# Layer 2's first gather moved ahead of its additions, radial features on another queue, and one ring for all stages

## The reference

```
h = relu(layernorm(x)); x = x + gat(h)         # layer 0: attention over in-edges and self loops
h = relu(layernorm(x)); x = x + sage_sage(h)   # layer 1: two SAGE convolutions (means over in-edges)
h = relu(layernorm(x)); x = x + layer2(h)
h = relu(layernorm(x)); x = x + relational(h)  # layer 3: typed messages, summed by dst

def layer2(h):
    radial, conical = h[:, :16], h[:, 16:32]
    rows, cols = concat([i, j]), concat([j, i])      # every edge in both directions
    agg = segment_sum(conical[cols], rows) / max(degree(rows), 1)
    return relu(concat([radial, agg]) @ W1 + b1) @ W2 + b2   # 32 -> 128 -> 32
```

## Time and profile before

| | |
|---|---|
| median of 3 runs | 4690.81 us |
| profiled execution | 4694.78 us |
| its span | 4693.0 us |
| GpSimd busy | 3469.0 us (74%) |
| VectorE busy | 2870.1 us (61%) |
| TensorE matmul busy | 2328.5 us (50%) |
| ScalarE busy | 958.4 us (20%) |
| stage f, from its first load to g's first gather | 3002.5 to 3604.6 us |

### The profile page before, as it was taken

One profiled execution on the slowest core, in us unless ns is written; L12 is line 12 of the kernel. 1 busy time (PEld: TensorE's weight loads), 2 busy tenths in 40 slices (PEclk: granted clock), 3 DMA queues, 4 the chain that ended last, 5 costly groups with the idle time before them and its releaser, 6 DMA issues. The chain is left out here.

```text
span 4693.0 us, 30595 instructions
## 1 busy us (share of the span) xinstructions
PE 2328.5 (50%) x8870; PEld 1409.5 (30%) x8870; DVE 2870.1 (61%) x3600; ACT 958.4 (20%) x1485; POOL 3469.0 (74%) x3151
## 2 busy tenths in 40 slices
PE   7820067775777730000622331177764677666562
PEld 3410034443555420000622331022221444443331
DVE  8866177775888756666311110166665899988783
ACT  0012022221445421111000000144442111111110
POOL 7777677774777747776588888777774777777777
PEclk9865555555989875555655555588886787877776
DMA  1035244441444432222122222344442111110100
GB/s 29 12 95 166 47 95 100 98 98 59 151 151 156 147 110 66 65 71 66 6 5 5 5 5 5 56 156 151 151 151 81 29 29 29 32 28 26 28 26 9
DMA packets 348969, 327.82 MB, mean 70 GB/s; under 512 B 223275, under 2 KB 295862, under 8 KB 347596
## 3 DMA queue, kind: packets, MB, share of 16 engines
q1 hardware_dynamic: 85600, 236.67, 14.0%
q0 software_dynamic: 144256, 45.62, 10.1%
q10 hardware_dynamic: 118944, 43.56, 3.9%
HBM read 170.38 MB, written 156.58 MB: 70 GB/s over the span
## 5 line engine op out<-in xcount | busy, mean ns | idle before, releaser
L1378 POOL DMA_INDIRECT sum_table<-e_add_rows,e_add_idx x392 | 612.7, 1563 | 142.4 <-issue 118.0
L536 POOL DMA_INDIRECT g_ring<-x_table,pos x392 | 412.3, 1052 | 173.7 <-issue 119.2
L536 POOL DMA_INDIRECT c_ring<-x_table,pos x392 | 398.9, 1018 | 175.8 <-issue 131.0
L1919 PE MATMUL g_pX<-w,g_h_T 128*128 128x512 f32 x784 | 438.2, 709 | 177.8 <-DVEq L1776 177.5
L536 POOL DMA_INDIRECT f_ring<-con_table,pos x392 | 419.3, 1070 | 134.5 <-issue 127.6
L1739 POOL DMA_INDIRECT out_x<-g_out_rows,end_index x392 | 426.7, 1088 | 119.5 <-issue 119.5
L536 POOL DMA_INDIRECT d_ring<-g_table,pos x392 | 389.4, 993 | 167.2 <-issue 124.0
L536 POOL DMA_INDIRECT b_ring<-h_table,src x392 | 405.9, 1035 | 132.9 <-issue 126.0
L345 POOL DMA_INDIRECT x_dst<-in_x,dst x392 | 400.3, 1021 | 134.2 <-issue 134.2
L1648 PE MATMUL f_pH<-f_T,w2in 128*128 128x448 f32 x672 | 319.8, 622 | 274.4 <-DVE f_T L1540 274.4
L1429 PE MATMUL e_pS<-e_values,e_equal 128*128 128x18 f32 x784 | 169.0, 378 | 379.8 <-DVEq L1403 379.8
(11 more groups left out here) (346 smaller groups left out, 5033.2 us busy)
## 6 DMA issues: line engine op xcount, KB each, us to landing
f_sums<-sum_table ACTq DMA_DIRECT2D x126, 238.0 KB
sum_table<-c_zero SPq DMA_DIRECT2D x39, 715.0 KB, 5.3
g_table<-c_g SPq DMA_DIRECT2D x42, 448.0 KB, 2.5
h_table<-a_xp SPq DMA_DIRECT2D x28, 560.0 KB, 3.7
a_x<-in_x SPq DMA_DIRECT2D x28, 448.0 KB, 5.9
b_h_node<-h_table ACTq DMA_DIRECT2D x28, 448.0 KB, 4.4
b_x_node<-in_x SPq DMA_DIRECT2D x28, 448.0 KB, 4.9
x_table<-b_x_node SPq DMA_DIRECT2D x28, 448.0 KB, 2.5
```

The lines of the kernel that those rows point to most:

```text
L536: pool.indirect_dma_start(out=ring[:, t, :], out_offset=None, in_=table, in_offset=bass.IndirectOffsetOnAxis(ap=idx[:, c * C + t:c * C + t ...
L1378: pool.indirect_dma_start(out=g.sums[b], out_offset=bass.IndirectOffsetOnAxis(ap=aidx[:, c % 2, t:t + 1], axis=0), in_=add[:, c % 2, t, :] ...
L1919: last = nc.tensor.matmul(pX[d % 2][:, j * 512:(j + 1) * 512], tsb[:, 0, quad], g.w3[:, (2 * d + j) % 4, :], start=True, stop=True)
```

## The change

`g.ring` is one ring for b, c, d, f and g; `ring_of(g, w)` is a view of it for rows of w values. Stage a's two spaces `edge0` and `endf` now lie in a tile that is used up. `gather_rows` takes a range of rows (`lo`, `hi`), and AHEAD is 5.

- Stage a: behind its own gathers, and ahead of the wait for them, GpSimd waits for the indices and for the node table's stores, and gathers rows 0 to 4 of b's chunk 0. b starts with row 5.
- Stage d: at its end GpSimd waits for the stores of layer 2's tables and gathers rows 0 to 4 of f's chunk 0. Stage e gathers rows 5 to 27 ahead of its additions, and rows 0 to 4 of chunk 1 behind them, ahead of the wait for them. f starts with row 5 of chunk 1.
- Stage f: the radial features of a node job are loaded on ScalarE's queue behind the three sums of the job, on the same semaphore, into a buffer chosen by the job's number. SP loads x alone, and the wait for x stands in `second`.

```diff
+AHEAD = 5
+def ring_of(g, w):
+    return g.ring[:, 0:2 * C * XW].rearrange("p (a k) -> p a k", a=2)[:, :, 0:C * w].rearrange("p a (t f) -> p a t f", f=w)
-def gather_rows(pool, table, ring, idx, c, sem):
-    for t in range(C):
+def gather_rows(pool, table, ring, idx, c, sem, lo=0, hi=C):
+    for t in range(lo, hi):
 ...
 # stage a, GpSimd
+            pool.wait_ge(src_here, 16)
+            for b in range(2):
+                pool.wait_ge(xp_stored[b], 16 * (NC // 2))
+            gather_rows(pool, g.XP, ring_of(g, XW)[:, 0], g.srcI, 0, g.rows["b"][0], hi=AHEAD)
             pool.wait_ge(rows, 16 * ET)
 ...
 # stage b, GpSimd
-                gather_rows(pool, g.XP, ring[:, c % 2], g.srcI, c, rows[c % 2])
+                gather_rows(pool, g.XP, ring[:, c % 2], g.srcI, c, rows[c % 2], lo=0 if c else AHEAD)
 ...
 # stage d, GpSimd
+            pool.wait_ge(ring_free, EC - 1)
+            for b in range(2):
+                pool.wait_ge(hn_stored[b], 32 * EC)
+                pool.wait_ge(ce_stored[b], 16 * (EC // 2))
+            gather_rows(pool, g.T2, ring_of(g, CON)[:, 0], g.posI, 0, g.rows["f"][0], hi=AHEAD)
 ...
 # stage e, GpSimd
+            gather_rows(pool, g.T2, ring_of(g, CON)[:, 0], g.posI, 0, g.rows["f"][0], lo=AHEAD)
             for c in range(EC):
 ...
+            gather_rows(pool, g.T2, ring_of(g, CON)[:, 1], g.posI, 1, g.rows["f"][1], hi=AHEAD)
             wait_added(pool, EC - 1)
 ...
 # stage f
+        def landed(j):
+            return 16 * sum(R + (kind == "n") for kind, _ in jobs[j % 2:j + 1:2])
-                sp.dma_start(flat(radn[:, k % 2]), node_rows(g.RN, k, CON)).then_inc(n_here[k % 2], 16)
-            for c in range(EC):
+            for c in range(1, EC):
                 if c > 1:
                     pool.wait_ge(ring_free, c - 1)
-                gather_rows(pool, g.T2, ring[:, c % 2], g.posI, c, rows[c % 2])
+                gather_rows(pool, g.T2, ring[:, c % 2], g.posI, c, rows[c % 2], lo=AHEAD if c == 1 else 0)
-                dve.wait_ge(here[b], 16 * R * (j // 2 + 1))
+                dve.wait_ge(here[b], landed(j))
-                    dve.wait_ge(n_here[k % 2], 32 * (k // 2 + 1))
-                    radial = radn[:, k % 2]
+                    radial = radn[:, b]
 ...
+                if kind == "n":
+                    dve.wait_ge(n_here[k % 2], 16 * (k // 2 + 1))
                 dve.wait_ge(out_sb, j + 1)
 ...
+                if kind == "n":
+                    act.dma_start(flat(radn[:, j % 2]), node_rows(g.RN, k, CON)).then_inc(here[j % 2], 16)
```

More of the change, by code:

```diff
@@ L257, in stage_tables @@
         xp = sb("xp", [P, 2, C, XW])
-        edge0 = sb("edge0", [P, ET])
-        endf = sb("outside", [P, ET])
+        endf, edge0 = dwf[:, 0, :], dwf[:, 2, :]
         own = sb("deg_run", [P, ET])
@@ L367, in edge_flags @@
                 nc.vector.tensor_copy(dwf[:], dwin[:])
-                nc.vector.memset(edge0[:], 1.0)
                 dve.drain()
@@ L373, in edge_flags @@
                 dve.drain()
+                nc.vector.memset(edge0, 1.0)
                 nc.vector.tensor_copy(g.same0[:], g.same[:])
@@ L376, in edge_flags @@
                 nc.vector.tensor_scalar(g.end[:], g.more[:], -1.0, 1.0, ALU.mult, ALU.add)
-                nc.vector.tensor_scalar(endf[:], g.more[:], float(OUTSIDE), None, ALU.mult)
+                nc.vector.tensor_scalar(endf, g.more[:], float(OUTSIDE), None, ALU.mult)
                 nc.vector.tensor_copy(chunks(own)[:, :, 0], chunks(g.same)[:, :, 0])
@@ L381, in edge_flags @@
                 nc.vector.memset(chunks(g.more0)[:, :, C - 1], 0.0)
-                nc.vector.tensor_tensor(endf[:], endf[:], dwf[:, 1, :], ALU.add)
+                nc.vector.tensor_tensor(endf, endf, dwf[:, 1, :], ALU.add)
                 dve.drain()
-                nc.vector.tensor_copy(g.endI[:], endf[:])
+                nc.vector.tensor_copy(g.endI[:], endf)
                 nc.vector.tensor_tensor_scan(g.pre[:], g.same0[:], own[:], 0.0, ALU.mult, ALU.add)
@@ L392, in edge_flags @@
                 dve.drain()
-                nc.vector.tensor_tensor_scan(own[:], g.same0[:], edge0[:], 0.0, ALU.mult, ALU.add)
+                nc.vector.tensor_tensor_scan(own[:], g.same0[:], edge0, 0.0, ALU.mult, ALU.add)
                 nc.vector.tensor_scalar(g.precut[:], g.pre[:], -NEG, NEG, ALU.mult, ALU.add)
@@ L549, in stage_attention @@
         w = g.norm
-        ring = sb("ring", [P, 2, C, XW])
+        ring = ring_of(g, XW)
         hd, prod, z = sb("h_dst", [P, 2, C, F]), sb("prod", [P, C, F]), sb("z", [P, C, F])
@@ L569, in stage_attention @@
         weight, own_weight, rden = (w.bank[:, at + 3 * F + k * C:at + 3 * F + (k + 1) * C] for k in range(3))
-        rows = [SW("rows0"), SW("rows1")]
+        rows = g.rows["b"]
         xn_here, hn_here, xn_stored = ([S(f"{x}{b}") for b in range(2)] for x in ("xn_here", "hn_here", "xn_stored"))
@@ L861, in stage_sage_first @@
         w = g.norm
-        ring, hs = sb("ring", [P, 2, C, F]), sb("h_src", [P, F, C])
+        ring, hs = ring_of(g, F), sb("h_src", [P, F, C])
         mask, run = sb("mask", [P, F, C]), sb("running", [P, F, C])
@@ L1201, in stage_sage_second @@
         w = g.norm
-        space = sb("ring", [P, EC * P + 1])
-        ring, crow = space[:, 0:2 * C * F].rearrange("p (a t f) -> p a t f", a=2, f=F), space[0:CON, :]
+        ring, crow = ring_of(g, F), g.ring[0:CON, C * CON:C * CON + EC * P + 1]
         mask, more, run, con = sb("mask", [P, F, C]), sb("mask_after", [P, CON, C]), sb("running", [P, F, C]), sb("con", [P, CON, C])
@@ L1459, in stage_third_layer @@
         R = len(g.sums)
-        ring, gm = sb("ring", [P, 2, C, CON]), sb("con_by_feature", [P, CON, C])
+        ring, gm = ring_of(g, CON), sb("con_by_feature", [P, CON, C])
         mask, run, own = sb("mask", [P, CON, C]), sb("running", [P, CON, C]), sb("own_sum", [P, C, CON])
@@ L1472, in stage_third_layer @@
         cr = Carry(nc, ctx, g, "f_sum", CON, pm[0:CON, 0:P], pm[:, P:P + CON])
-        rows = [SW(f"rows{b}") for b in range(2)]
+        rows = g.rows["f"]
         here, n_here, n_stored = ([S(f"{x}{b}") for b in range(2)] for x in ("here", "n_here", "n_stored"))
@@ L1697, in stage_relations @@
         w = g.norm
-        ring, xf = sb("ring", [P, 2, C, F]), sb("x_full", [P, C, F])
+        ring, xf = ring_of(g, F), sb("x_full", [P, C, F])
         h = (sb("h_src", [P, C, F]), sb("h_dst", [P, C, F]))
@@ L1973, in build @@
         g.norm = Norm(nc, g)
+        g.ring = sb("ring", [P, 2 * C * XW + 1])
+        g.rows = {stage: [g.lasting(f"{stage}_rows{a}") for a in range(2)] for stage in "bf"}
         with ExitStack() as early:
```

## The result

The changed kernel takes 4659.9 us (median of 4 runs, 4658.8 to 4662.3), the kernel before on the same chip 4690.9 (4 runs): a ratio of 0.9936, 95% interval 0.9921 to 0.9952, some 30 us. The forecast was 4666, in a range of 4646 to 4690, and faster.

A forecast was written before the change was run, and what follows sets the result against it. GpSimd's instructions bound layers 0, 1, 3 and layer 2's additions; in stage f VectorE waits, chiefly for radial features. 4694.8 - 1.3 + 10.5 + 4.9 - 9.2 - 29.3 = 4670.4, less 4.0, about 4666 us; range 4646 to 4690.

The forecast's parts named there:

- Layer 0's border: Border of the tables and layer 0: five rows ahead of the wait bring b's sixth row earlier, -1.3 us.
- The 28 rows: Border of the second SAGE layer and the additions: 28 rows gathered ahead delay the first addition, +10.5 us.
- The five rows behind the additions: Border of the additions and stage f: five rows ahead of the drain delay f's start, +4.9 us.
- Chunk 0: Start of stage f: VectorE's ring wait of 9.74 us goes, ScalarE's extra issues cost 0.5; together -9.2 us.
- The pace: Stage f without the radial wait: 13 periods of 38.1 us instead of 40.38, -29.3 us.
- TensorE starts on it: Stage f, edge job: from transposed input to TensorE's first output product, 6.3 to 7.8 us, mean 7.0.
- VectorE's part: Stage f, each period: from VectorE taking an output to the edge job's input transposed, mean 16.3 us.
- product to next output: Stage f, each period: 13.25 us from TensorE's first output product through the next node job's last, plus ScalarE's 1.5.
- its bound for slow chunks: Stage f: if TensorE's start took 7.8 us in all chunks, the gain would be only -18 us.
- B: Rival, stage f: radial lands when needed or later behind the three sum loads, losing the 29.3; 4696 us, chance 0.11.
- C: Rival, stage f: ScalarE becomes the chain, 28 added issues cost 12.0 us; 4708 us, chance 0.09.
- A: Rival, stage f: TensorE keeps its faster clock level, then GpSimd binds; -58 us in f, 4647 us, chance 0.14.

The follow-up runs named there:

- radial alone: Against the kernel before, only the radial loads move (and the ring is one), all gathers ahead taken out; 4666.7 us, ratio 0.9955.

## Why the prediction came out as it did

**Layer 0's border.** Predicted -1.3, measured -1.13 (12.89 for 14.02). The drain follows the new rows and ends at 546.0, 0.9 before the sixth row, as reckoned from d's border.

**The 28 rows.** Predicted +10.5, measured +10.77. The parts, each counted from d's last gather: five rows start 26.04 after it (predicted 26.25), the stage's first instruction stands at 37.27 (predicted 37.0), the first addition at 66.98 (predicted 66.70). The 23 rows took 29.06, 0.3 over 23 x 1.25, where 0.5 was allowed.

**The five rows behind the additions.** Predicted +4.9, measured +4.99.

**Chunk 0.** Predicted -9.2, measured -9.22 (27.10 for 36.32). That it fits so closely is partly luck: the four kernels with all 33 rows ahead have 26.03 to 27.10 there.

**The pace.** Predicted 13 periods of 38.1, measured 37.72: -34.6 instead of -29.3. This is the term that was mis-sized, and within it one step: "TensorE starts on it [...] mean 7.0". It measured 6.5 as a mean; the others came out as said, VectorE's part 16.2 (16.3) and product to next output 14.88 (14.75), each a mean without chunk 0. I had averaged the start over quick and slow chunks of before (6.3 and 7.8); after, it is 6.3 to 6.9, with a granted clock of 0.86 over the stretch where the earlier trace rows has 0.83. The clock is what makes the difference: the mean granted clock within the starts is 0.67 before and 0.72 after, and 4.7 over these is 7.0 and 6.5. So the mechanism, the chain that stands behind the radial wait, was right; the prediction held the start for a fixed price, where it is work at a granted clock that differs from kernel to kernel and from chunk to chunk. Some 7 of the 34.6 us (13 times 7.05 - 6.51) come from there, which the prediction did not foresee. Two slips of its working change little: 16.3 is the mean of twelve chunks and not thirteen, and its bound for slow chunks is 29.3 - 13 x 0.8 = 19, not 18.

**Where the sum stands.** The steps come to -1.1 + 10.8 + 5.0 - 9.2 - 34.6 and -0.8 behind the last read = -30 (the table), as the comparison has it. The spans of the two profiles differ by 35.1. The other 5 lie in stages that the change leaves alone, such as 3.98 us in stage a ahead of its border: d's last gather started at 2192.9 to 2208.1 in the eight kernels, which up to there differ only in the ring and flags that share their space and in the border of a and b (1.1 us). So one execution's landmark tells a step only against another one close by. Taken from the profiled execution minus 4.0, the forecast had 24.4 of 30: 4666 for 4660.

**The rivals.** B (radial comes back behind the sums) fell: no radial wait. By the Trainium skill's rule that it leaned on, "Issuing engines are not separate DMA queues" in "DMA: Bandwidth & Descriptors", another issuer buys only issue time; radial on SP's own queue, loaded earlier, did as well as on ScalarE's, so the rule is not contradicted: it was the place in the order that counted, for radial and for x. C (ScalarE the chain) fell: of its idle time ahead of the hidden activations 260.3 us are left (last line below; 293.8 before), so the 28 issues fit in. A (GpSimd binds) is not what happened, since its last row of f starts at 3514.49, 19.2 us before the last read, and where a read waited for its row (radial alone) it began 3.7 after the row's start; but without the 33 rows it does bind, and with 18 nearly. The prediction did give the 33 rows as the reason that GpSimd does not bind, but its sum prices them as chunk 0's 9.2 alone. In the pace the radial move gives 20.1 without them (525.0 to 504.9) and 31.4 with them (521.8 to 490.4).

```profile
L1634 ACT ACTIVATE f_hid_T<-f_pH,b2col 128x448 f32<-128x448 f32 x336 | 204.8, 637 | 260.3 <-PE f_pH L1672 247.2
```

## What to carry to other kernels

Work moved ahead is free only up to the idle time that it fills: read that idle time in the row of the instruction that ends it (23.21 us, 18 rows) and move no more; the fifteen rows beyond it, ten of them on two borders, cost 15.8 us here. When a wait goes, price what stands behind it, here a chain over three engines (37.7 us a chunk) and GpSimd, which needs 28 x 1.375 = 38.5 and binds unless it starts ahead; then two edits that give 21 and nothing apart give 30 together. A chain that gets shorter on paper has to be measured part by part: here two edits shortened one part as forecast, and TensorE's start, at a lower granted clock, got longer by as much.

## What was not expected of the hardware

The time of work that no edit touches moved by up to 15 us between single executions of these kernels (d's last gather at 2192.9 to 2208.1; 13.7 us between two of the four on one chip), much more than the distances between neighbouring rows of GpSimd did (the last destination gather to b's sixth row: 12.87 to 12.89 in six kernels). What sets the spread was not looked into.
